# A four-layer network kernel: both scales of the ternary layers in one chain, and an opening that waits for two batches' tokens

## What is computed

```python
x = x + _L0_xattn_ref(_layernorm(x, axis=-1), ctx_512, ctx_512, ...)
...
x = x + _L3_ffn_ref(_layernorm(x, axis=-1), L3_ffn_W1, L3_ffn_b1, L3_ffn_W2, L3_ffn_b2)
```

```python
def bitlinear(x, W, b):
    w_scale = jnp.clip(jnp.mean(jnp.abs(W)), EPS, None)
    Wq = clip(round(W / w_scale), -1, 1) * w_scale
    x_scale = jnp.clip(jnp.max(jnp.abs(x), axis=-1, keepdims=True), EPS, None)
    xq = clip(round(x * (QB / x_scale)), -QB - 1, QB) * (x_scale / QB)
    return jnp.einsum('bnd,hd->bnh', xq, Wq) + b
h = jax.nn.gelu(bitlinear(x, W1, b1), approximate=False)     # 128 -> 512
return bitlinear(h, W2, b2)                                  # 512 -> 128
```

## Time and profile before

| | us |
|---|---|
| median of 3 runs (lowest, highest) | 2518.63 (2516.05, 2523.42) |
| the profiled execution | 2544.34 |
| its span, first to last instruction | 2542.60 |
| TensorE, matmuls busy | 2192.1 (86%) |
| VectorE busy | 1813.8 (71%) |
| ScalarE busy | 1335.9 (53%) |
| GpSimd busy | 1245.5 (49%) |

### The profile page before, as it was taken

One profiled execution on the slowest core, in us unless ns is written; L12 is line 12 of the kernel. 1 busy time (PEld: TensorE's weight loads), 2 busy tenths in 40 slices (PEclk: granted clock), 3 DMA queues, 4 the chain that ended last, 5 costly groups with the idle time before them and its releaser, 6 DMA issues. The chain is left out here.

```text
span 2542.6 us, 67314 instructions
## 1 busy us (share of the span) xinstructions
PE 2192.1 (86%) x22345; PEld 1689.5 (66%) x22352; DVE 1813.8 (71%) x4650; ACT 1335.9 (53%) x2821; POOL 1245.5 (49%) x1940
## 2 busy tenths in 40 slices
PE   5878997999988768779999997899888999998855
PEld 4557995666656557657777776666667888885523
DVE  5975554666659754578888867677698866667977
ACT  2434552343434435535555556444476888883456
POOL 4546635555534357277777745333164333324333
PEclk9968998999999869989999998999989999999978
DMA  8022211000000213200000000000000312210000
GB/s 310 10 110 74 77 53 29 14 12 12 12 2 1 78 57 97 78 18 13 9 10 9 9 2 20 10 1 0 15 5 5 92 57 66 58 47 14 1 9 25
DMA packets 82031, 96.69 MB, mean 38 GB/s; under 512 B 16720, under 2 KB 61136, under 8 KB 79760
## 3 DMA queue, kind: packets, MB, share of 16 engines
q1 hardware_dynamic: 73616, 77.12, 9.6%
q0 software_dynamic: 8192, 16.79, 2.3%
HBM read 56.51 MB, written 37.36 MB: 37 GB/s over the span
## 5 line engine op out<-in xcount | busy, mean ns | idle before, releaser
L1722 DVE TENSOR_TENSOR l2f_h_lo<-l2f_h,l2f_h_hi 128x512 fp32r<-128x512 f32 x256 | 187.5, 764 | 100.8 <-ACT l2f_h_hi L1643 100.7
L1012 POOL TENSOR_TENSOR a_pm<-a_pt,tri_post 128x256 f32<-128x256 f32 x256 | 179.6, 730 | 87.2 <-ACT a_pt L668 86.7
L808 DVE TENSOR_REDUCE l1s_negm<-l1s_s 128x6 bf16<-128x768 f32 x128 | 123.1, 961 | 109.2 <-PE l1s_s L485 109.1
L1650 ACT ACTIVATE l2f_h<-l2f_f,ahead 128x512 f32<-128x512 f32 x256 | 174.3, 688 | 49.6 <-DVE l2f_h_lo L1722 32.5
L808 DVE TENSOR_REDUCE a_negm<-a_s 128x4 bf16<-128x1024 f32 x128 | 156.1, 1219 | 32.0 <-PE a_s L485 30.3
L668 ACT ACTIVATE l1s_pt<-l1s_st 128x768 f32<-128x768 f32 x128 | 96.9, 811 | 155.5 <-PE l1s_st L523 155.5
L1817 POOL TENSOR_TENSOR l2f_acc<-l2f_tmp,l2f_acc 128x512 f32<-128x512 f32 x56 | 73.0, 1303 | 207.2 <-DVE l2f_tmp L1740 207.2
L1643 ACT ACTIVATE l2f_h_hi<-l2f_h 128x512 fp32r<-128x512 f32 x256 | 154.5, 633 | 0.0
L668 ACT ACTIVATE a_pt<-a_st 128x1024 f32<-128x1024 f32 x128 | 126.5, 1065 | 3.3 <-PE a_st L523 3.3
L684 ACT ACTIVATE a_q_hi<-a_pa 128x256 fp32r<-128x256 f32 x64 | 24.5, 383 | 185.0 <-PE a_pa L451 185.0
L1534 PE MATMUL l2f_f<-l2f_x_hi,l2f_w_hi 128*128 128x512 f32 x256 | 101.9, 398 | 1.2 <-POOL l2f_w_lo L1804 1.2
(11 more groups left out here) (575 smaller groups left out, 7076.4 us busy)
## 6 DMA issues: line engine op xcount, KB each, us to landing
expert_rows<-zeros SPq DMA_DIRECT2D x16, 1056.0 KB, 17.5
l2f_wrow<-weights_by_expert SPq DMA_DIRECT2D x64, 256.0 KB, 3.2
l0f_w<-in_l0f_w SPq DMA_DIRECT2D x8, 640.0 KB
l0f_x_in_sb<-expert_rows SPq DMA_DIRECT2D x72, 64.0 KB
expert_rows<-l0f_y SPq DMA_DIRECT2D x72, 64.0 KB, 1.6
l1f_x_in_sb<-expert_rows SPq DMA_DIRECT2D x72, 64.0 KB
expert_rows<-l1f_y SPq DMA_DIRECT2D x72, 64.0 KB
ahead<-in_l2f_w SPq DMA_DIRECT2D x6, 512.0 KB, 4.5
```

What stands on the lines that cost most here:

```text
L808: dve.tensor_reduce(dst, src, AX.X, ALU.max, negate=True).then_inc(max_done, 1)
L1012: last = pool.tensor_tensor(pm[:, par, heads_, kt, :], pt[:, par, heads_, kt * (T + P):kt * (T + P) + P], K["tri_post"][:].unsqueeze(1).br ...
L1650: act.activation(h[:, j], psum_f[j][:], ACT.Gelu, bias=col(e, j)).then_inc(h_ready, 1)
L1722: dve.tensor_tensor(h_lo[:, pos % 2, j], h[:, j], h_hi[:, pos % 2, j].bitcast(F32), ALU.subtract)\
```

## The change

In the opening stage: the load of `x` is divided. The tokens of the first two batches go first, the rest behind the attention's weights and with a semaphore of its own (`arrived`), which only VectorE's statistics of batch 2 in the first attention wait for. VectorE does its fills ahead of the normalisation, and the wait for the masks last; GpSimd computes `rstd` in the middle of the selects; ScalarE does one activation on a column before it waits for the transposes.

In the ternary stage: the maxima of h (s) and of x (s+3) are taken one behind the other into a two-row tile `most`, and clip, reciprocal, scale and back scale are one instruction each for both (`clipped`, `inverse`, `scaling`, `back`). The order of a step becomes
- VectorE: statistics, aggregate (s+4); maximum of h (s), maximum of x (s+3), clip, reciprocal, scale, rounding of h, rounding of x, back scale; output (s-1).
- GpSimd: `shift` (s+4), `diag` (s+3), addition (s-1).
- TensorE: `pt` (s-1), `ph` (s+1), `px` (s+2), `po` (s-1).
- ScalarE: `hq_t` (s-1), gelu (s+1), copy of `px` (s+2), `xn` (s+4), `hq` (s), `xq` (s+3).

The weights' back scale is written in two instructions, in the order of the rows.

```diff
-            sp.dma_start(x[:], a["x"].rearrange("b (t p) d -> p (b t) d", p=P)).then_inc(in_loaded, 16)
+            rows = a["x"].rearrange("b (t p) d -> p (b t) d", p=P)
+            first = slice(0, 2 * TT)
+            rest = slice(2 * TT, NT)
+            sp.dma_start(x[:, first, :], rows[:, first, :]).then_inc(in_loaded, 16)
             sp.dma_start(ctx_t[0:CK, :], a["ctx_t"]).then_inc(in_loaded, 16)
             fetch(sp, K, None, after)
+            sp.dma_start(x[:, rest, :], rows[:, rest, :]).then_inc(K["arrived"], 16)
             sp.wait_ge(in_loaded, 32)
...
             for t in range(CTILES):
                 last = dve.bn_aggr(mv[:, t, :], st6[:, t, :])
             last.then_inc(stats, 1)
-            dve.wait_ge(step, MASK_STEPS)
-            dve.tensor_reduce(K["own_slot"][:], K["slots4_8"][:].rearrange("p (u q) -> p u q", u=4), AX.X, ALU.add)\
-                .then_inc(filled, 1)
-            dve.wait_ge(filled, 2)
-            dve.wait_ge(rstd_ready, 1)
-            for t in range(CTILES):
-                last = dve.tensor_scalar(cn[:, t, :], c[:, t, :], mv[:, t, 0:1], rstd[:, t:t + 1],
-                                         ALU.subtract, ALU.mult)
-            last.then_inc(cn_ready, 1)
             dve.memset(ctx_t[CK:P, :], 0.0).then_inc(zeroed, 1)
             dve.memset(ctx_n[CK:P, :], 0.0)
             dve.wait_ge(zeroed, 1)
             dve.memset(ctx_t[CK:CK + 1, :], 1.0).then_inc(zeroed, 1)
             dve.memset(zeros[:], 0.0).then_inc(zeroed, 1)
             dve.wait_ge(zeroed, 3)
+            dve.wait_ge(rstd_ready, 1)
+            for t in range(CTILES):
+                last = dve.tensor_scalar(cn[:, t, :], c[:, t, :], mv[:, t, 0:1], rstd[:, t:t + 1],
+                                         ALU.subtract, ALU.mult)
+            last.then_inc(cn_ready, 1)
+            dve.wait_ge(step, MASK_STEPS)
+            dve.tensor_reduce(K["own_slot"][:], K["slots4_8"][:].rearrange("p (u q) -> p u q", u=4), AX.X, ALU.add)\
+                .then_inc(filled, 1)
+            dve.wait_ge(filled, 2)
...
+            pool.wait_ge(stats, 1)
+            pool.tensor_scalar(veps[:], mv[:, :, 1], EPS, None, ALU.add).then_inc(veps_ready, 1)
+            pool.wait_ge(veps_ready, 1)
+            pool.tensor_tensor(rstd[:], veps[:], K["half"][:, 0:CTILES], ALU.pow).then_inc(rstd_ready, 1)
             v = K["own1_8"][:].rearrange("p a (l e d) -> p a l e d", l=2, e=2)
...
-            pool.wait_ge(stats, 1)
-            pool.tensor_scalar(veps[:], mv[:, :, 1], EPS, None, ALU.add).then_inc(veps_ready, 1)
-            pool.wait_ge(veps_ready, 1)
-            pool.tensor_tensor(rstd[:], veps[:], K["half"][:, 0:CTILES], ALU.pow).then_inc(rstd_ready, 1)
...
+            act.activation(warm[:], g[:], ACT.Identity)
...
+                if clear and isinstance(b, int) and b == 2:
+                    dve.wait_ge(K["arrived"], 16)
...
-                link(dve.tensor_scalar(wq[:], ws[:], 1.0 / QB, None, ALU.mult))
+                for i in range(2):
+                    link(dve.tensor_scalar(wq_by_part[:, i:i + 1], ws[:, 1 - i:2 - i], 1.0 / QB, None, ALU.mult))
...
-            def rounded(src, a, c, r, s, out, chain, at0, freed):
-
-                k = [0]
-
-                def step(ins):
-                    k[0] += 1
-                    ins.then_inc(chain, 1)
-                    dve.wait_ge(chain, at0 + k[0])
-
-                step(dve.tensor_reduce(a[:], src, AX.X, ALU.max, apply_absolute_value=True))
-                step(dve.tensor_scalar(c[:], a[:], EPS, None, ALU.max))
-                step(dve.reciprocal(r[:], c[:]))
-                step(dve.tensor_scalar(s[:], r[:], QB, None, ALU.mult))
-                freed()
-                for t in range(G):
-                    last = dve.tensor_scalar(out[:, t], src[:, t], s[:, t:t + 1], ROUND, ALU.mult, ALU.add)
-                return last
-
-            def scale_of(dst, c, i):
-
-                return dve.tensor_tensor(dst, c[:], wq[:, i:i + 1].broadcast_to([P, G]), ALU.mult)
+            def rounded(n, pn, q, pq):
+
+                has_h, has_x = inside(n), inside(q)
+                part = slice(0 if has_h else 1, 2 if has_x else 1)
+                if has_h:
+                    dve.wait_ge(h_ready, G * n + G)
+                    dve.tensor_reduce(most[:, 0, :], h[:, pn % 2], AX.X, ALU.max, apply_absolute_value=True)\
+                       .then_inc(qstep, 1 if has_x else 2)
+                if has_x:
+                    dve.wait_ge(xn_ready, q + 1)
+                    dve.tensor_reduce(most[:, 1, :], xn[:, pq % 2], AX.X, ALU.max, apply_absolute_value=True)\
+                       .then_inc(qstep, 1 if has_h else 2)
+                dve.wait_ge(qstep, QS * q + 2)
+                dve.tensor_scalar(clipped[:, part], most[:, part], EPS, None, ALU.max).then_inc(qstep, 1)
+                dve.wait_ge(qstep, QS * q + 3)
+                wait(dve, diag_ready, q - 1 if has_x else N)
+                dve.reciprocal(inverse[:, pq % 2, part], clipped[:, part]).then_inc(qstep, 1)
+                dve.wait_ge(qstep, QS * q + 4)
+                dve.tensor_scalar(scaling[:, part], inverse[:, pq % 2, part], QB, None, ALU.mult).then_inc(qstep, 1)
+                dve.wait_ge(qstep, QS * q + 5)
+                if has_h:
+                    wait(dve, hq_ready, n)
+                    for t in range(G):
+                        last = dve.tensor_scalar(hi[:, t], h[:, pn % 2, t], scaling[:, 0, t:t + 1], ROUND, ALU.mult, ALU.add)
+                    last.then_inc(hi_ready, 1)
+                if has_x:
+                    wait(dve, xq_ready, q)
+                    for t in range(G):
+                        last = dve.tensor_scalar(xi[:, t], xn[:, pq % 2, t], scaling[:, 1, t:t + 1], ROUND, ALU.mult, ALU.add)
+                    last.then_inc(xi_ready, 1)
+                    wait(dve, h_ready, G * (q - 3))
+                if has_h:
+                    wait(dve, o1_ready, n - 3)
+                rows = part.stop - part.start
+                dve.tensor_tensor(back[:, pq, part], clipped[:, part],
+                                  wq_by_part[:, part].unsqueeze(2).broadcast_to([P, rows, G]), ALU.mult).then_inc(qstep, 1)
...
             def emit(at):
                 k, pk = at(4)
@@ -2783,14 +2805,6 @@
                     for t in range(G):
                         last = dve.bn_stats(st6[:, t, :], src[:, t, :])
                     last.then_inc(lstep, 1)
-                n, pn = at(0)
-                if inside(n):
-                    dve.wait_ge(h_ready, G * n + G)
-                    rounded(h[:, pn % 2], ha, hc, hr, hs, hi, hstep, HS * n,
-                            lambda: wait(dve, hq_ready, n)).then_inc(hi_ready, 1)
-                    wait(dve, o1_ready, n - 1)
-                    scale_of(hd[:, pn % 2], hc, 1).then_inc(hstep, 1)
-                if inside(k):
                     dve.wait_ge(lstep, k + 1)
                     wait(dve, shift_ready, k - 1)
                     dve.sem_inc(K["passed"], 1)
@@ -2799,24 +2813,20 @@
                     last.then_inc(stats, 1)
                     dve.wait_ge(stats, k + 1)
                     dve.sem_inc(K["passed"], 1)
+                n, pn = at(0)
+                q, pq = at(3)
+                if inside(n) or inside(q):
+                    rounded(n, pn, q, pq)
                 l, pl = at(-1)
                 if inside(l):
                     dve.wait_ge(o_done, l + 1)
-                    dve.wait_ge(hstep, HS * l + HS)
+                    dve.wait_ge(qstep, QS * (l + 3) + QS)
                     wait(dve, added, l - 1)
                     for t in range(G):
                         last = dve.scalar_tensor_tensor(out=o1[:, pl % 2, t], in0=psum_o[:, t, :],
-                                                        scalar=hd[:, pl % 2, t:t + 1], in1=b2b[:],
+                                                        scalar=back[:, (pl + 3) % PER, 0, t:t + 1], in1=b2b[:],
                                                         op0=ALU.mult, op1=ALU.add)
                     last.then_inc(o1_ready, 1)
-                q, pq = at(3)
-                if inside(q):
-                    dve.wait_ge(xn_ready, q + 1)
-                    wait(dve, diag_ready, q - 1)
-                    rounded(xn[:, pq % 2], xa, xc, xr[:, pq % 2], xs, xi, xstep, XS * q,
-                            lambda: wait(dve, xq_ready, q)).then_inc(xi_ready, 1)
-                    wait(dve, h_ready, G * (q - 3))
-                    scale_of(xd[:, pq, :], xc, 0).then_inc(xstep, 1)
...
-                q, pq = at(3)
-                if inside(q):
-                    pool.wait_ge(xstep, XS * q + 3)
-                    wait(pool, h_done, G * (q - 3))
-                    pool.sem_inc(K["passed"], 1)
-                    o = [P, G, P]
-                    pool.tensor_tensor(diag[:, pq], K["ident"][:].unsqueeze(1).broadcast_to(o),
```

(74 more changed lines are left out.)

20 lines of the change are left out of this document (8 added, 12 removed).

## The result

| | before | after |
|---|---|---|
| median of 19 runs each, same set, us | 2520.28 (2514.05 to 2524.22) | 2512.54 (2508.01 to 2517.94) |
| ratio | | 0.9973 [0.9965, 0.9981] |
| profiled execution: span, mean clock | 2542.6, 0.941 | 2509.5, 0.943 |

The kernel became 0.27% faster: 6.8 us, by the interval 4.8 to 8.8. I had forecast 2501.6 with 2497 to 2511, a gain of 17.0. The two traces are therefore compared stage by stage only. In the sets of runs of the experiments the kernel before took 2542.8, 2546.6 and 2545.2, so every ratio is taken inside its own set.

The account below looks back on a forecast made before the run. The prediction took VectorE's order to end the opening and VectorE to bound the ternary stage at full TensorE clock. Gains of 11.9 (loop), 0.6 (fill) and 4.5 (opening) made 17.0 us off 2518.63: 2501.6, range 2497 to 2511.

Parts of the forecast that it names:

- VectorE's step: Ternary stage: one VectorE step falls from 6.56 to 5.76 us, bounds 5.65 and 6.19.
- ScalarE's round with TensorE: Ternary stage: the new round from `pt` to `pt` at full clock takes 5.63 us; the wait for `shift` stays hidden.
- 11 x 5.75: Ternary loop: eleven rounds at 5.75 us plus a shorter step 12 make 68.2 for 80.1, minus 11.9.
- the first rival: Ternary stage: TensorE's clock falls; three to seven low steps (2509 to 2518 us) 8 in 100, more 4 in 100.
- The price of a low round: Ternary stage: at low clock a round takes 8.16 us, each low step taking 2.4 of the 17.0 us gain.
- Fill: Start of the ternary stage: `shift` before `diag` brings `xn` earlier, minus 0.6 us, between 0 and 1.2.
- Drain: End of the ternary stage, behind step 12: h alone as before, no gain.
- Opening: Stage before the first attention: ends at 17.2 for 21.69 us, minus 4.5, bounds 5.4 and 3.0.
- Rivals 2 and 3: Ternary VectorE gets other stretches, 2510.6 us, 12 in 100; opening gives nothing, 2506.1 us, 6 in 100.
- The lengthening beside `diag`: Ternary VectorE step: `diag` now meets the rounding of h instead of x; the sum of both roundings left unchanged.
- The profiled execution: Whole kernel: profiled 2544.34 us, 25.7 above the runs' median 2518.63; the same 17.0 us gain taken off the median.

Follow-up runs that it names:

- awake_after: Changed kernel plus 24 idle TensorE products per step behind `po`; ratio to the kernel before 0.9919.
- no_bias_awake: Changed kernel without the first layer's bias product, plus 36 idle products per step behind `po`; ratio to the kernel before 0.9898.
- mid_3: Changed kernel plus 3 idle products per step in the middle of TensorE's hole, by a wait for `xn`; ratio to the kernel before 0.998.
- awake_12: Changed kernel plus 12 idle TensorE products per step behind `po`; ratio to the kernel before 0.9906.
- awake_before: Kernel before plus 24 idle TensorE products per step ahead of the wait for `pt`; ratio to the kernel before 0.9987.
- after_again: The changed kernel run once more, nothing altered; ratio to the kernel before 0.9962.
- ternary_only: Changed ternary stage with the opening of the kernel before; ratio to the kernel before 0.9993.
- opening_only: Changed opening with the ternary stage of the kernel before; ratio to the kernel before 0.9987.
- one_load: Changed kernel with the tokens loaded in one transfer again; ratio to the kernel before 0.9968.

## Why the prediction was wrong, point by point

**VectorE's step.** Forecast 5.76, measured 5.59 in the step shown and 5.63 in the mean of `awake_after`. The joint scales, the aggregate's wait (0.65 for 0.63) and the clip without its stretch came as counted. From the first rounding to the back scale, with the second rounding between, it is 1.63, as the two roundings took before. The 0.17 by which 5.76 is too long lies in small gaps that the sum left out, behind the maximum of h, the aggregate and the back scale.

**ScalarE's round with TensorE.** Forecast 5.63, measured 5.62. `xn` never waited for `shift`. With both loops at 5.6 and step 12 at 4.86, the loop would have been 11 x 5.62 + 4.86 = 66.7: 13.4 gained where I took 11.9. `no_bias_awake` shows that VectorE's loop is not shorter than some 5.5 by itself, so the two are nearly as equal as I took them.

**The step that failed** is the term 11 x 5.75, which has every round at full clock: the eleven rounds took 75.00, 6.82 each. It rests on the weighing of the first rival, TensorE's clock: "before the low step TensorE had been idle 3.15 us; after a gap of 2.84 it stayed at full clock", and so "the gap falls to 2.4" and the clock was to hold. The gap did fall, to 2.29, and the mean granted clock of the rounds was 0.82. Two single gaps were read as a rule on their length, and they carried none. The trace of the kernel before already spoke against it: its step 0 follows a hole of 1.98, and that round ran at 0.74. `mid_3` with holes of 1.26 and 0.69 lost the clock, `awake_12` with 1.62 kept it.

Nor had I asked what the low clock cost the old order, though the 80.1 that I subtracted from ran at a mean of 0.85. TensorE has the same 3.33 of work in a full round of both kernels, and about 5.0 where the mean clock is 0.74 to 0.79. In the old order VectorE's step of 6.6 covers a round that is slow for a part: the two of 0.74 in `awake_before` took 6.57, like those beside them, and behind the first round only those of 0.62 cost, about 7.7 for 6.6. In the first round VectorE has less to do, and there 0.74 cost the kernel before 6.55 for the 5.34 of `awake_before`. The new chain is 0.8 shorter, and a round with 5.0 of TensorE's work takes 7.06 to 7.39. The clock stayed nearly as it was, and the new order made the loop depend on it: from `pt` of step 0 to step 12, the 24 products are worth 13.0 us to the new order (79.86 to 66.82) and 3.7 to the old one (80.10 to 76.38).

The Trainium skill has a like case of another kernel in "TensorE: Matmul & The Clock Gate", section "A second HAM failure mode: psum-queue depth-cycling": a TensorE that idles briefly but often between groups of matmuls has a clock that goes up and down. The trace agrees in kind: with a hole in every round the clock went up and down in both kernels. I had cited another part of that page for the opposite.

**The price of a low round** was mis-sized in that rival: 2.4 to 2.5 forecast, 1.65 measured (13.2 over eight). I had priced a round wholly at 1.2 GHz, and the low rounds have a mean of 0.77: about half of each is low. By my price eight low rounds would have given 2520.8; with 1.65 each the same sum gives 2514.8, and with the loop at full clock 1.5, the fill 0.7 and the opening 0.4 better than forecast 2512.2. As a gain this is 6.4, for 6.8 by the runs. That 2512.2 also lies next to the median of 2512.54 is in part luck, since the kernel before moved from 2518.63 to 2520.28 between its two sets. To the case of eight or more low rounds I gave 4 in 100, to within 0.3% 9.

**Fill.** Forecast 0.6, bounds 0 and 1.2, measured 1.31. The new order's fill repeats (23.21, 23.22 in `after_again`, 23.24 in `ternary_only`), the old one's does not (24.52, 25.82 in `opening_only`), so by the second pair it is 2.6. Why is open. **Drain.** Nothing, as said.

**Opening.** Forecast 4.5, measured 4.93. The normalisation began at 11.71 for the forecast 11.7 and ended at 14.21 for 14.5; `context_n` ended at 16.99 for 17.2. Beside the selects it took 2.50 for the earlier trace rows's 1.87: 0.63 more, about a quarter of the 2.4 that I had as the most. The late tokens and their wait cost nothing, and `one_load` adds that the division gave nothing either.

**Rivals 2 and 3** did not occur: no small scale was stretched, and the opening gave all of its gain in the trace. The lengthening beside `diag` only changed its partner. In the kernel before the rounding of h, with no `diag` beside it, stands so on VectorE's timeline:

```profile
2452.28 0.88 DVE L2772 TENSOR_SCALAR l3f_hi<-l3f_h,l3f_hs 128x512 f32<-128x512 f32 x2
```

It became 1.31, 0.43 more, and the rounding of x fell from the 0.91 of the earlier trace rows to 0.47. The lock of a whole GpSimd instruction, 0.61, of which the Trainium skill speaks in "SBUF — State Buffer", section "Who interferes with whom", does not show in full here: the row has about two thirds of it.

**The profiled execution** stood 25.7 above the median of the runs, and I took the sum off the median. That held: the ratios of the two sets with this kernel, 6.8 us [4.8, 8.8] and 9.7 [5.9, 13.5], hold the 6.5 of the stages, and the difference of the two spans does not.

## What to carry to other kernels

A shorter chain around the same TensorE work can make a loop depend on TensorE's clock. List, round by round, the granted clock and TensorE's busy time before the change, and ask which engine's work covers the low parts now and whether it still will. Price the loop with the mean clock that it already has (here 0.84 before and 0.82 after), never with two single gaps. Idle products and the shorter chain were worth something only together: 24 products alone gave 3.3 us, the new order alone 1.8, and `awake_12`, at 0.9906, gave 2.5 times the gain of the same kernel without them, 0.9962 in the same set. A divided load is worth something only if the load ends the stage.

## What the runs showed of the hardware

- TensorE's clock fell in loops with a hole of 2.29 in a full round of 5.62 and with holes of 1.26 and 0.69, and stayed full with one of 1.62 and 12 products more. In the old order with 24 products it fell twice in eleven rounds of 6.46, behind a hole of 1.94 the first time.
- Two traces of the changed kernel have the same pattern of full and low rounds, to 0.05 us a round.
- Nearly the same mean clock, 0.84 and 0.82, cost the old order about 3.7 us of its loop and the new one 13.0, by what 24 products gave back.
- At 1.2 GHz nearly throughout (PEclk 0.53) the loop without the bias product took 5.49 a round, where the loop with it took 5.62 at full clock.
- With the small activation in front, ScalarE's table load ran at 0.80, ahead even of that activation's wait for its data (4.23); in the kernel before it ran behind the waits, at 17.25.
- SP's issue of the context transfer took 5.66 behind the whole tokens' transfer (`one_load`) and 0.52 behind that of two batches.
